# A table of the token in each slot: experts gather their rows by it and scatter finished rows to the output

## The chip, the cores and the metric

The kernel runs on one core of one Trainium2 chip. The metric is the device time of one execution in microseconds (us); the median of several executions stands for a kernel. The engines are PE (TensorE), DVE (VectorE), ACT (ScalarE), POOL (GpSimd) and SP (SyncE). SP, ACT and POOL issue DMAs. Each engine works through its own instructions in order; semaphores tie them together.

## What is computed

A layer norm of x (1250 tokens x 768), then a graph attention network (three layers, four heads) and a linear attention over the same rows; both are added to x. The change touches only what follows, a routed feed-forward layer with eight experts (F = 384):

```python
xf = layernorm(x)                                  # 1250 x 768
probs = softmax(xf @ switch_w + switch_b)          # 8 experts
prob_max, routes = max(probs), argmax(probs)
capacity = int(1.25 * N / E)                       # 195 rows an expert
rank = place of the token in its expert, by falling prob_max
keep = rank < capacity
buf[routes, rank] = xf where keep                  # 8 x 195 rows
h = gelu(buf @ w1 + b1)
o = h @ w2 + b2
y = where(keep, o[routes, rank], xf)
x = x + y * prob_max
```

## The kernel before, in words

The program is written by hand in Bass. A list `ORDER` holds (name, index) steps; each engine runs through the whole list and emits what it has to do for a step. So `ORDER` sets the order on every engine and in every DMA queue, and a wait holds up all that stands behind it on its engine. A class `Waits` leaves out waits that an engine has already passed.

The tokens are NT = 10 tiles of up to 128 rows (the last has 98). The part that matters is `last_order`. Its first part runs over the tiles in ticks, several steps of different tiles in each. In tick i SP loads `ar` (a row tile of the graph network, `row_in`) for tile i, and at i = 2, 5 and 8 also the weights `w1_in`, `w2_in` (1152 KB each) and the bias `b2_in` (384 KB) of experts 0, 1 and 2; then it loads `mi` (384 KB, `new_x`) for tile i-2. For tile t = i-2, PE ends a product in two halves (`row_mm`), DVE adds them up (`row_add`, L1477), adds `mi` (`new_x`, L1492, result in `x2`, which shares its place with `wacc`), takes mean and variance, and writes the normed row tile `xf` (L1517). PE turns `xf` in the next tick (`f_turn`, L1053) for the router (`logits`, L1062; `route`; `rank`, L1558 to L1569, which compares each token with all earlier tiles).

After the last tile comes the second part. `ranked` (L1574 to L1594) makes ten-column tables on DVE: `slot[:, 0]`, the row of `slot_rows` to which each token goes (a spare row when the expert is full), and `slot[:, 1]`, the row of `expert_rows` from which its result comes. `dispatch` has POOL scatter the ten `xf` tiles by indirect DMA into `slot_rows` in HBM (L1974), while DVE adds the token's own share to `x2` (L1599). When all ten have landed, SP loads `slot_rows` back in 13 tiles of 120 rows (`slots_in`, L2224), PE turns them (`slots_turn`, L1092), ACT evicts the low half and DVE the high half into `sT_low`, `sT_high`, and then the experts run.

For expert e, PE computes `hidden(e)` (L1104, 18 fp32 products of 195 columns), ACT applies gelu, and PE then computes `expert_out(e-1)` (L1116, 12 fp32 products of 384 columns). DVE adds b2 into `orow` (L1617), and ACT's queue stores `orow` to `expert_rows` (L1883). One or two slot tiles are turned between `expert_out(e-1)` and `hidden(e+1)`. After the last expert, `fetch` has POOL gather a row for each token from `expert_rows` (L1982); DVE scales it and adds `x2` (L1625), and SP stores the ten tiles to the output (L2228). `slot_zero` (L1888) zeroes `slot_rows` once, much earlier, on ACT's queue.

## Time and profile before

| | |
|---|---|
| median of 3 runs | 1821.16 us (1818.88 to 1825.3) |
| the profiled execution | 1823.74 us |
| its span, first to last instruction | 1822.0 us |
| PE busy | 1586.4 us (87%) |
| DVE busy | 1170.8 us (64%) |
| mean granted TensorE clock | 0.945 |

The span is what the views of the trace are measured in; 1.74 us of the execution lie outside it. The chain of work that ended last goes by 70% through PE and by 16% through DVE. The change touches the last 320 us only, so this text reads those: from 1501 us (the ticks), from 1633 us (ranking done, dispatch), from 1660 us (experts) and from 1792 us (fetch and output) to the end at 1822 us. The share of busy time over the whole span tells little about them.

### The profile page before, as it was taken

Reading aid. Unit: us, or ns where it says so; the run is one execution under the profiler, and the core shown is the slowest. Engines: PE = TensorE matmul, PEld = TensorE weight load, DVE = VectorE, ACT = ScalarE, POOL = GpSimd, SP = SyncE. Lnnn points to the kernel's source line nnn. Section 1 sums busy time; section 2 is a strip of 40 time slices with the busy share of each in tenths; the row PEclk is TensorE's granted clock in tenths of the full one; section 3 lists DMA queues with packets and bytes.
Section 4 is the critical chain, followed back from the end, with each engine's and each line's share of the span. In section 5 each row is a group of like instructions: output and inputs, shape, how many; then the busy total and the mean of one; then the engine's idle time right before and its main releaser. Section 6 shows DMA issues by size and latency. Waiting matters only on the chain.

```text
span 1822.0 us, 24680 instructions
## 1 busy us (share of the span) xinstructions
PE 1586.4 (87%) x9602; PEld 1205.0 (66%) x9663; DVE 1170.8 (64%) x2517; ACT 647.3 (36%) x1254; POOL 515.8 (28%) x282
## 2 busy tenths in 40 slices
PE   3799999999997787999998699969999998855993
PEld 2456666556565665988888688868889875534661
DVE  7677553024434697898879999968769725771113
ACT  2231111122224766766665333344324413421110
POOL 1387787777730000111211212121212210001002
PEclk9899999999998988999999899989999999967997
DMA  7424434454424315222263443444124116317615
GB/s 220 125 40 115 104 80 113 66 92 108 74 59 163 101 65 177 82 63 82 92 161 102 138 146 113 140 147 136 50 85 143 53 51 218 113 67 246 203 57 195
DMA packets 197361, 208.90 MB, mean 115 GB/s; under 512 B 83040, under 2 KB 152814, under 8 KB 197244
## 3 DMA queue, kind: packets, MB, share of 16 engines
q1 hardware_dynamic: 117453, 183.36, 30.9%
q0 software_dynamic: 76416, 14.38, 6.6%
q10 hardware_dynamic: 3375, 9.59, 2.0%
q8 instruction: 76, 1.25, 0.3%
q14 instruction: 41, 0.34, 0.1%
HBM read 140.67 MB, written 66.22 MB: 114 GB/s over the span
## 4 chain that ended last, share of the span: by engine, by line
PE 70%; DVE 16%; DMA 4%; ACT 4%; issue 3%; POOL 1%; SPq 1%; ACTq 0%; POOLq 0%; DVEq 0%
PE bank L959 17%; PE bank L805 13%; PE bank L806 13%; PE bank L804 12%; PE bank L1116 3%; PE bank L1104 3%; DVE eb L1386 3%; DVE eb L1395 2%; PE bank L984 2%; DVE junk L1349 2%; PE bank L1012 2%; ACT ef L1777 1%; PE bank L906 1%; DVE q_max L1418 1%; PE bank L1027 1%
## 5 line engine op out<-in xcount | busy, mean ns | idle before, releaser
L959 PE MATMUL bank<-hb,eb 128*128 128x193 f32 (+3 forms) x2400 | 431.3, 337 | 41.0 <-DVE eb L1395 36.0
L959 PEld LDWEIGHTS bank<-hb,eb 128*128 128x128 f32 (+3 forms) x2400 | 411.3, 195 | 53.8 <-DVE eb L1395 40.6
L1939 POOL DMA_INDIRECT table<-amount,place x170 | 342.9, 2017 | 157.7 <-DMA table<-amount,place 68.7
L1950 POOL TENSOR_TENSOR node<-node,rinv 128x960 f32<-128x960 f32 (+2 forms) x36 | 62.6, 1752 | 821.4 <-DVE rinv L1408 821.4
L1386 DVE SCALAR_TENSOR_TENSOR eb<-shift_b,as_low,shift_b 128x640 f32<-128x640 f32 (+1 forms) x240 | 231.4, 1004 | 6.9 <-DMA shift_b<-shift_rows 6.9
L1747 ACT ACTIVATE eb<-eb,asd 128x640 f32<-128x640 f32 (+1 forms) x240 | 182.6, 815 | 136.9 <-DVE eb L1386 136.9
L1395 DVE SCALAR_TENSOR_TENSOR eb<-eb,count 128x1280 f32<-128x1280 f32 (+1 forms) x120 | 200.1, 1668 | 0.0
L1349 DVE CUSTOM_DVE_ANT_0 junk<-ab,absent 128x1250 bf16<-128x1250 f32 x120 | 174.8, 1456 | 1.3
L804 PE MATMUL bank<-w_o_hi,aT_hi 128*128 128x384 bf16 (+1 forms) x360 | 120.1, 334 | 0.4 <-DVE won L1562 0.4
L805 PE MATMUL bank<-w_o_lo,aT_hi 128*128 128x384 bf16 (+1 forms) x360 | 119.8, 333 | 0.0
L806 PE MATMUL bank<-w_o_hi,aT_lo 128*128 128x384 bf16 (+1 forms) x360 | 119.7, 332 | 0.0
L804 PE MATMUL bank<-wg_hi,x1T_hi 128*128 128x384 bf16 (+3 forms) x360 | 117.9, 328 | 0.0
L806 PE MATMUL bank<-wg_hi,x1T_lo 128*128 128x384 bf16 (+3 forms) x360 | 117.9, 327 | 0.0
L805 PE MATMUL bank<-wg_lo,x1T_hi 128*128 128x384 bf16 (+3 forms) x360 | 117.8, 327 | 0.0
L1956 POOL TENSOR_TENSOR node<-node,bgh 128x960 f32<-128x960 f32 (+2 forms) x36 | 79.6, 2225 | 1.9
L1617 DVE TENSOR_TENSOR orow<-bank,b2r 105x384 f32<-105x384 f32 (+1 forms) x32 | 17.8, 556 | 94.8 <-PE bank L1116 94.8
L1777 ACT ACTIVATE ef<-bank,q_shift 128x256 f32<-128x256 f32 (+1 forms) x120 | 50.6, 476 | 73.0 <-DVE q_shift L1423 73.0
L805 PE MATMUL bank<-xnT_lo,wq_hi 128*128 128x512 bf16 (+1 forms) x210 | 70.8, 337 | 3.7 <-DVE wq_lo L1194 2.8
L806 PE MATMUL bank<-xnT_hi,wq_lo 128*128 128x512 bf16 (+1 forms) x216 | 73.0, 338 | 0.3
L1304 DVE TENSOR_REDUCE kmax<-bank 128x1 f32<-128x512 f32 (+1 forms) x60 | 40.2, 692 | 49.1 <-PE bank L806 49.1
L804 PE MATMUL bank<-xnT_hi,wq_hi 128*128 128x512 bf16 (+1 forms) x204 | 68.6, 336 | 0.0
L1012 PEld LDWEIGHTS bank<-context,qf 128*128 128x128 f32 (+1 forms) x480 | 61.5, 204 | 10.1 <-ACT att L1814 3.8
(272 smaller groups left out, 2854.4 us busy)
## 6 DMA issues: line engine op xcount, KB each, us to landing
w<-in_w SPq DMA_DIRECT2D x16, 1152.0 KB, 6.2
shift_b<-shift_rows SPq DMA_DIRECT2D x24, 625.0 KB, 6.2
h_rows<-h_row SPq DMA_DIRECT2D x27, 388.0 KB
hb<-h_rows SPq DMA_DIRECT2D x12, 873.0 KB
ar<-node_rows SPq DMA_DIRECT2D x27, 384.0 KB, 3.2
qk_rows<-qk_row SPq DMA_DIRECT2D x12, 625.0 KB
ab<-as_rows SPq DMA_DIRECT2D x12, 625.0 KB, 5.6
stage<-in_W SPq DMA_DIRECT2D x18, 384.0 KB, 4.7
```

The lines of the kernel that those rows point to most:

```text
L804: T.matmul(out_ap, lhs[0], rhs[0], start=first, stop=False, skip_group_check=skip)
L805: T.matmul(out_ap, lhs[0], rhs[1], start=False, stop=False, skip_group_check=skip)
L806: return T.matmul(out_ap, lhs[1], rhs[0], start=False, stop=last, skip_group_check=skip)
L959: ins = T.matmul(bank[w // 2][0:M, c0:c0 + GC + 1], p[0:K, u, w * P:w * P + M], hv[0:K, t, 0:GC + 1], start=opens and u == 0 and w % 2 == ...
L1012: ins = T.matmul(ov[0:R, u, hh, :], qf[q % 4][:, hh * MT + m, 0:R], context[:, m, hh, :], start=u == 0 and hh == 0 and m == 0, stop=m == M ...
L1349: V.tensor_tensor_reduce(out=junk[0:R, :], in0=ab[lh % 2][0:R, :], in1=absent[0:R, t, :], scale=1.0, scalar=-BIG, op0=ALU.add, op1=ALU.max ...
L1386: ins = V.scalar_tensor_tensor(eb[i % EDGE_BUFFERS][:, u, 0:w], low, as_low[:, t, lh:lh + 1], high, ALU.add, ALU.max)
L1395: V.scalar_tensor_tensor(e, e, 1.0, count[:, 2 * pair:2 * pair + 2, ns], ALU.min, ALU.mult).then_inc(sem["edge_w"], 1)
L1747: ins = A.activation(e[:, u, 0:w], e[:, u, 0:w], ACT.Exp, bias=asd[:, t, 8 * l + hh:8 * l + hh + 1])
L1777: ins = A.activation(ef[g % 4][0:R, hh, :], bank[3 + g % 2][0:R, hh * FEATS:(hh + 1) * FEATS], ACT.Exp, bias=bias)
L1939: G.indirect_dma_start(tables[i], bass.IndirectOffsetOnAxis(place[:, c:c + 1], axis=0), amount16[:, c:c + 1], None, compute_op=ALU.add).th ...
L1956: ins = G.tensor_tensor(v, v, bgh[lh % 2][0:R, :].unsqueeze(1).broadcast_to([R, ws.stop - ws.start, GC]), ALU.add)
```

## The change

A table in PSUM now says which token sits in each slot. DVE makes two 0/1 masks, `on_row` (128 x 10 x 105: is the token's place within its half expert this row) and `on_tile` (128 x 10 x 16: which of the 16 half experts), and multiplies the second by the token's number less 4096 and by its probability. PE multiplies and adds up over the ten tiles (`map`), which gives, for each of 105 rows and 16 half experts, the token's number less 4096 and its gate, or zeros. DVE turns these into `from_row` (clipped to a valid row), `to_row` (out of range for an empty slot) and `gate` (`mapped`).

`xf` and `x2` of each tile are stored to HBM as soon as they exist (`rows_out`, two 384 KB DMAs on SP a tile, in the tick's list behind `mi`). POOL gathers the rows of half an expert at a time straight from `xf_rows` (`slots_in`), later their `x2` rows (`base_in`), and scatters the finished rows to the output (`expert_out`). Tokens without a slot are covered by storing all of `x2` with its own share to the output first (`own`). DVE gets one more pass for each half expert. Slot tiles are now 105 and 90 rows, 16 in place of 13. The loads of the weights of experts 3 and 4 move behind `hidden(0)` in the list. `slot_zero`, `dispatch` and `fetch` are gone.

```diff
@@ last_order
+        yield "rows_out", t
...
-    yield "w1_in", 3
-    yield "w2_in", 3
-    yield "ranked", 0
-    for t in range(NT):
-        yield "dispatch", t
-    for t in range(4):
-        yield "slots_in", t
-    yield "w1_in", 4
-    yield "w2_in", 4
+    for name in ("ranked", "map", "mapped"):
+        yield name, 0
+    own = iter(range(NT))
+    for j in range(4):
+        yield "slots_in", j
+        yield "own", next(own)
     for e in range(EXPERTS + 1):
         if e < EXPERTS:
+            for j in range(2 * e, 2 * e + 2):
+                yield "slots_turn", j
+                if j + 4 < SLOT_TILES:
+                    yield "slots_in", j + 4
+                for t in itertools.islice(own, 3):
+                    yield "own", t
             yield "hidden", e
+            if e == 0:
+                for i in range(3, WEIGHT_SETS):
+                    yield "w1_in", i
+                    yield "w2_in", i
+            for j in range(2 * e, 2 * e + 2):
+                yield "base_in", j
...
@@ PE
+            def map_(_):
+                pe.wait_ge("slotted", 10)
+                pe.wait_ge("row_sum", 2 * NT * (LAYERS + 1))
+                for t in range(NT):
+                    R = rows(t)
+                    ins = T.matmul(bank[5][0:WIDEST, 0:2 * SLOT_TILES], on_row[0:R, t, :], in_tile[0:R, t, :],
+                                   start=t == 0, stop=t == NT - 1)
+                ins.then_inc(sem["map_mm"], 1)
...
@@ DVE
+                V.tensor_tensor(on_row[:, :, :], iota_row[:, :].unsqueeze(1).broadcast_to([P, NT, WIDEST]),
+                                pm[:, 5, :].unsqueeze(2).broadcast_to([P, NT, WIDEST]),
+                                ALU.is_equal).then_inc(sem["slotted"], 1)
...
+            def mapped(_):
+                at_tile, share = bank[5][0:WIDEST, 0:SLOT_TILES], bank[5][0:WIDEST, SLOT_TILES:2 * SLOT_TILES]
+                ve.wait_ge("map_mm", 1)
+                V.tensor_scalar(from_row[0:WIDEST, :], at_tile, NOWHERE + 0.25, N - 0.75, ALU.add,
+                                ALU.min).then_inc(sem["mapped"], 1)
+                V.tensor_scalar(to_row[0:WIDEST, :], at_tile, NOWHERE + 0.25, None, ALU.add).then_inc(sem["mapped"], 1)
+                V.tensor_copy(gate[0:WIDEST, :], share).then_inc(sem["mapped"], 1)
...
+                    V.scalar_tensor_tensor(orow[o][0:n, :], orow[o][0:n, :], gate[0:n, j:j + 1], base_row[j % 4][0:n, :],
+                                           ALU.mult, ALU.add).then_inc(sem["ended"], 1)
...
@@ POOL
+            def slots_in(j):
...
+                G.indirect_dma_start(sr[j % 4][0:n, :], None, xf_rows,
+                                     bass.IndirectOffsetOnAxis(from_row[0:n, j:j + 1], axis=0)
+                                     ).then_inc(sem[f"slots_in{j % 4}"], 16)
+
+            def base_in(j):
+                n = slots_of(j)[2]
+                ge.wait_ge("own_out", 16 * NT)
+                ge.wait_ge("ended", j - 3)
...
+            def expert_out(e):
+                for j in range(2 * e, 2 * e + 2):
+                    n = slots_of(j)[2]
+                    ge.wait_ge("mapped", 2)
+                    ge.wait_ge("ended", j + 1)
+                    G.indirect_dma_start(out, bass.IndirectOffsetOnAxis(to_row[0:n, j:j + 1], axis=0),
+                                         orow[j % OUT_ROWS][0:n, :], None, bounds_check=N - 1, oob_is_err=False
+                                         ).then_inc(sem[f"expert_out{j % OUT_ROWS}"], 16)
...
@@ SP
+            def rows_out(t):
+                R = rows(t)
+                sy.wait_ge("xf_ready", t + 1)
+                S.dma_start(xf_rows[at(t), :], xf[0:R, t, :]).then_inc(sem["rows_out"], 16)
+                S.dma_start(x2_rows[at(t), :], x2[0:R, t, :]).then_inc(sem["rows_out"], 16)
```

SP's queue at the tick that loads expert 1's weights. Before (`ar_99` is tile 5's, `w_1` the two weights, the last row tile 3's `mi`):

```order
L2164 DMA ar_98<-node_rows 128x768 [waits turned]
L2219 DMA mi_153<-mixed_rows 128x768 [waits x2]
L2164 DMA ar_99<-node_rows 128x768 [waits turned]
L2200 DMA w_1_219<-in_w 128x6x384
L2207 DMA w_1_220<-in_w 128x3x768
L2212 DMA b2r_223<-in_b 128x768
L2219 DMA mi_154<-mixed_rows 128x768 [waits x2]
```

And now:

```order
L2255 DMA mi_159<-mixed_rows 128x768 [waits x2]
L2260 DMA xf_rows<-xf 128x768 [waits xf_ready]
L2261 DMA x_rows<-wacc 128x768
L2202 DMA ar_103<-node_rows 128x768 [waits turned]
L2236 DMA w_1_229<-in_w 128x6x384
L2243 DMA w_1_230<-in_w 128x3x768
L2248 DMA b2r_233<-in_b 128x768
L2255 DMA mi_160<-mixed_rows 128x768 [waits x2]
```

The loads of a tick now stand behind a store that waits for `xf` of tile t-1, and `mi` of tile t is the last of them.

DVE around expert 1's rows and the slot copies that follow them. Before:

```order
L1617 TENSOR_TENSOR orow_239<-bank,b2r_223 105x384 [waits out2_mm,b2_in1]
L1617 TENSOR_TENSOR orow_239<-bank,b2r_223 105x384 [waits out2_mm]
L1617 TENSOR_TENSOR orow_240<-bank,b2r_223 90x384 [waits out2_mm] x2
L1605 COPY sT_high<-bank 128x3x120 [waits slots_turned] x2
```

And now:

```order
L1657 TENSOR_TENSOR orow_249<-bank,b2r_233 105x384 [waits out2_mm,b2_in1]
L1657 TENSOR_TENSOR orow_249<-bank,b2r_233 105x384 [waits out2_mm]
L1663 SCALAR_TENSOR_TENSOR orow_249<-orow_249,gate,base_row_115 105x768 [waits base_in2,expert_row]
L1657 TENSOR_TENSOR orow_250<-bank,b2r_233 90x384 [waits out2_mm] x2
L1663 SCALAR_TENSOR_TENSOR orow_250<-orow_250,gate,base_row_116 90x768 [waits base_in3,expert_row]
L1645 COPY sT_high<-bank 128x3x105 [waits slots_turned]
L1645 COPY sT_high<-bank 128x3x90 [waits slots_turned]
```

A full-width pass now stands between the last `orow` addition and the first slot copy, and there are always two slot copies.

## Rows read from the trace of the kernel before

**Rows 1.** Chain of waits, 1500 to 1560 us: start, us, what
```profile
1501.42 0.32 SPq L2164
...
1514.06 0.97 DVE wacc L1492
...
1518.57 1.51 PE bank L1053 x6
...
1524.59 0.97 DVE wacc L1492
```

**Rows 2.** Timeline of DVE, 1495 to 1634 us: x2 added, xf written
```profile
1528.27 0.68 DVE L1517 TENSOR_SCALAR xf<-wacc,stats 128x768 f32<-128x768 f32 x1
1534.23 0.96 DVE L1492 SCALAR_TENSOR_TENSOR wacc<-wacc,mi 128x768 f32<-128x768 f32 x1
1537.91 0.68 DVE L1517 TENSOR_SCALAR xf<-wacc,stats 128x768 f32<-128x768 f32 x1
1544.40 0.96 DVE L1492 SCALAR_TENSOR_TENSOR wacc<-wacc,mi 128x768 f32<-128x768 f32 x1
1568.98 0.68 DVE L1517 TENSOR_SCALAR xf<-wacc,stats 128x768 f32<-128x768 f32 x1
1576.14 0.96 DVE L1492 SCALAR_TENSOR_TENSOR wacc<-wacc,mi 128x768 f32<-128x768 f32 x1
```

**Rows 3.** Timeline of SP's DMA issues, tick that loads expert 2's weights
```profile
1556.05 0.32 SPq L2164 DMA_DIRECT2D ar<-node_rows  x1
```

**Rows 4.** Tile mi, issue to landing: load issued at 1515.05, then at 1558.01 us
```profile
DMA to landing us min/median/max: 2.8/2.8/2.8
...
DMA to landing us min/median/max: 8.9/8.9/8.9
```

**Rows 5.** Windows: length, PE, PEld, DVE, ACT, POOL busy, PEclk, DMA share, GB/s
```profile
1562.00:1564.00 2.00, 2.00 (x14) 1.18 (x13) 1.42 (x5) 1.01 (x1) 0.00 (x0) 1.00 1.03 418
1754.00:1756.00 2.00, 2.00 (x8) 2.00 (x7) 0.00 (x0) 0.00 (x0) 0.00 (x0) 0.50 0.01 5
```

**Rows 6.** Chain of waits, 1560 to 1822 us
```profile
1623.41 2.02 PE bank L1062 x12
...
1633.02 0.20 DVE pm L1574
...
1649.54 3.34 DMA slot_rows<-xf,slot
...
1660.20 8.67 PE bank L1104 x36
...
1677.48 7.75 PE bank L1116 x24
...
1686.74 6.21 PE bank L1104 x36
1692.95 7.75 PE bank L1116 x24
...
1703.82 6.18 PE bank L1104 x36
...
1753.46 7.86 PE bank L1104 x36
...
1776.79 15.49 PE bank L1116 x48
...
1808.41 7.96 DMA sr<-expert_rows,slot
```

**Rows 7.** Timeline, 1629 to 1825 us
```profile
1634.89 9.38 DVE L1599 SCALAR_TENSOR_TENSOR wacc<-xf,pm,wacc 128x768 f32<-128x768 f32 x10
1635.14 1.68 POOL L1974 DMA_INDIRECT slot_rows<-xf,slot  x1 [143.84 <-DVE pm L1594]
...
1796.30 1.00 POOL L1982 DMA_INDIRECT got<-expert_rows,slot  x1 [145.80 <-DMA expert_rows<-orow]
...
1800.25 1.02 DVE L1625 SCALAR_TENSOR_TENSOR got<-got,pm,wacc 128x768 f32<-128x768 f32 x1 [7.39 <-DMA got<-expert_rows,slot]
```

More of the change, by code:

```diff
@@ L424, in last_order @@
                 yield "b2_in", e - 1 + 3
-    for t in range(NT):
-        yield "fetch", t
 def whole_order():
@@ L502, in program @@
         attn_rows = dram("attn_rows", (N, D))
[L503 to L504 removed]
+        xf_rows = dram("xf_rows", (N, D))
+        x2_rows = dram("x2_rows", (N, D))
         base = 16512
@@ L544, in program @@
         pm = put("pm", [P, 8, NT])
-        slot = put("slot", [P, 2, NT], U32)
         b1c = put("b1c", [128, EXPERTS, KF])
@@ L553, in program @@
         b2r = [put("b2r0", [128, D])]
+        iota_row = put("iota_row", [P, WIDEST])
+        to_row, from_row = (put(name, [P, SLOT_TILES], U32) for name in ("to_row", "from_row"))
+        gate = put("gate", [P, SLOT_TILES])
         assert cursor[0] <= after_count
+        cursor[0] = at_logits
+        iota_i = put("iota_i", [P, WIDEST], I32)
         r_a = cursor[0] = after_count
@@ L572, in program @@
         cursor[0] = r_a
-        w1_3, w2_3 = put("w1_3", [128, KD, F]), put("w2_3", [128, KF, D])
-        sr = [put(f"sr{i}", [P, D]) for i in range(4)]
+        sT_high = put("sT_high", [128, KD // 2, SLOTS])
+        sr = [put(f"sr{i}", [P, D]) for i in range(3)]
         assert cursor[0] <= r_b
@@ L580, in program @@
         r_c = cursor[0]
+        cursor[0] = r_b
+        base_row = [put(f"base_row{i}", [P, D]) for i in range(4)]
         cursor[0] = r_b
@@ L712, in program @@
         assert cursor[0] <= over
-        cursor[0] = r_d
-        got = [put(f"got{i}", [P, D]) for i in range(6)] + sr
-        assert cursor[0] <= after_features
+        cursor[0] = r_zero
+        sr.append(put("sr3", [P, D]))
         identP = ident[0:P, 0:P]
@@ L1633, in vector_program @@
                         expert_setup=expert_setup, new_x=new_x, new_norm=new_norm, logits=logits, route=route,
-                        rank=rank, ranked=ranked, dispatch=dispatch, slots_turn=slots_turn,
-                        expert_out=expert_out, fetch=fetch_)
+                        rank=rank, ranked=ranked, mapped=mapped, own=own_, slots_turn=slots_turn,
+                        expert_out=expert_out)
             for name, *where in ORDER:
@@ L1968, in expert_setup @@
                                 pattern=[[-1, P]], channel_multiplier=1).then_inc(sem["pool_set"], 1)
-            def dispatch(t):
-                R = rows(t)
-                ge.wait_ge("slotted", 10)
-                ge.wait_ge("slot_zeroed", 16)
-                G.indirect_dma_start(slot_rows, bass.IndirectOffsetOnAxis(slot[0:R, 0, t:t + 1], axis=0),
-                                     xf[0:R, t, :], None).then_inc(sem["to_slots"], 16)
-            def fetch_(t):
-                R = rows(t)
-                for o in range(OUT_ROWS):
-                    ge.wait_ge(f"expert_out{o}", 16 * (2 * EXPERTS // OUT_ROWS))
-                ge.wait_ge("hid_mm", KF * EXPERTS)
-                G.indirect_dma_start(got[t][0:R, :], None, expert_rows,
-                                     bass.IndirectOffsetOnAxis(slot[0:R, 1, t:t + 1], axis=0)
-                                     ).then_inc(sem[f"fetch{t}"], 16)
+            def slots_in(j):
+                n = slots_of(j)[2]
+                ge.wait_ge("rows_out", 32 * NT)
+                ge.wait_ge("mapped", 1)
+                ge.wait_ge("slots_turned", 2 * (j - 3))
+                G.indirect_dma_start(sr[j % 4][0:n, :], None, xf_rows,
+                                     bass.IndirectOffsetOnAxis(from_row[0:n, j:j + 1], axis=0)
+                                     ).then_inc(sem[f"slots_in{j % 4}"], 16)
@@ L1986, in gpsimd_program @@
             mine = dict(edges_in=edges_in, place=place_, finish=finish,
-                        expert_setup=expert_setup, dispatch=dispatch, fetch=fetch_)
+                        expert_setup=expert_setup, slots_in=slots_in, base_in=base_in, expert_out=expert_out)
             for name, *where in ORDER:
@@ L2238, in sync_program @@
                     mine[name](*where)
-            sy.wait_ge("result_out", 16 * NT)
+            sy.wait_ge("own_out", 16 * NT)
+            for o in range(OUT_ROWS):
+                sy.wait_ge(f"expert_out{o}", 16 * (SLOT_TILES // OUT_ROWS))
         block = ctx.enter_context(nc.Block())
```

157 lines of the change are left out of this document (76 added, 81 removed).

## The prediction

> **What bounds the kernel now.** I read the page's chain first (PE 70%), then the chain of waits, the timeline and the windows of the last 320 us, since the change touches nothing before. There are four stretches, each with another bound.
>
> In the ticks (1501 to 1620 us) DVE and PE hand work to each other and neither has slack: x2 of a tile, xf, PE's turn, the ranking, the next product. Whatever delays x2 delays everything. The reader should see that this happens once already: `mi` of tile 0 stands behind expert 0's weights in SP's queue, its tick began with an issue at 1501.42 and DVE got the tile at 1514.06, 12.5 us later; PE turned xf at 1518.57 [rows 1]. At expert 2's tick issue to landing took 1556.05 to 1558.01 + 8.9 = 1566.9, that is 10.9 us [rows 3, 4], but nobody waited: the tile was needed at 1576.14 [rows 2].
>
> From 1633.0 the dispatch is a single file: tables, ten scatters, a landing, a load, turns, then `hidden(0)` at 1660.2 [rows 6]. From there PE bounds with gaps between experts, up to 1776.79 + 15.49 = 1792.3 [rows 6]. Then 29.7 us of fetch and output up to 1822.0, in which PE does nothing.
>
> **The end: -24.0 us.** Now, after PE's last product: DVE's addition of 0.6, one more pass (the same form over 768 columns took 1.02 [rows 7]), a hand-over of 0.3 (DVE's tables to POOL's first scatter), then one indirect scatter of 90 rows. The last scatter of before took 3.34 us from the start of its instruction to landing [rows 6]. Sum 0.6 + 1.0 + 0.3 + 3.4 = 5.3, with 0.4 for the end of the program 5.7 against 29.7: -24.0. Bounds: the scatter lands in 2.5 or in 5.0 us, so -25 to -22.5.
>
> **The dispatch: -9.7 us.** From the tables' start at 1633.0 [rows 6]: six small DVE steps, 1.1 us; the mask of 1050 columns 1.2 us (768 columns took 0.96, so 1.25 ns a column [rows 2]); three shorter passes, 0.8 us; ten products for the table. Twelve records of six router products took 2.02 us at the low clock [rows 6], 0.34 us each, so 3.4 us for ten. Then `from_row` and the hand-over, 0.6. POOL starts its first gather at 1640.1. The first gather of before was used 3.95 us after its start (1796.30 to 1800.25 [rows 7]), so rows are there at 1644.1. The turn takes 1.5, the second tile comes 1.3 to 1.9 later. What bounds then is DVE, in its order: own shares 0 to 3, slot copy 0, own shares 4 to 6, slot copy 1. An own share costs 0.94 (9.38 for ten [rows 7]), so copy 0 ends at 1646.4, the three shares at 1649.2, copy 1 at 1649.8. With a little for gathers that meet the 3.8 MB of stores of the own shares, `hidden(0)` starts at 1650.5 in place of 1660.2. Bounds -11 to -8.
>
> **The first product: +1.0 us.** `hidden(0)` took 8.67 where others take 6.2 [rows 6], because PE came out of a wait at 1.2 GHz. Before, 3.6 us of turns ran without a break ahead of it; now they are thinner and DVE makes PE wait 2 to 3 us after them. I take +1.0; bounds 0, and all of it at the low clock, 12.4, so +3.7.
>
> **The gaps between experts: +6.6 us.** Before, a gap with one slot tile is 1677.48 + 7.75 = 1685.23 to 1686.74, 1.5 us; with two it is 1692.95 + 7.75 = 1700.70 to 1703.82, 3.1 us [rows 6]. There were three of each among the six: 13.9 us. ACT's wait for its store, which held up its slot copy, is gone. But on DVE the added pass stands between the last `orow` and the first slot copy: 0.6 + 1.0 + 0.5, then the second tile's high half is turned, 0.6, and copied, 0.45, with hand-overs 3.4 us, and every gap has two tiles. Six times 3.4 is 20.5: +6.6, bounds +5 to +8. POOL's three DMAs a half expert, 48 of 1.0 to 1.7 us [rows 7], lie beside 110 us of products; base rows are asked for a whole expert ahead, so nobody waits.
>
> **The clock in the gaps: +1.7 us.** One gap of three of 3.1 us was followed by a fall to the low clock (0.50 at 1754 to 1756 [rows 5]): 7.86 in place of 6.2 [rows 6]. Six gaps at one in three give two falls, one more than before. Bounds: no fall, -1.7, and six, +8.3.
>
> **The ticks: +16.9 us.** This is the part that speaks against the change. `mi` of tile t now stands behind the two stores of tile t-1, so it can't be asked for before xf of t-1 is written; before, tile 6's was asked for at 1558.01, 11.6 us ahead of that and 18 us before its use [rows 2, 4]. What is left is the time from the end of xf to the next L1492: 1538.59 to 1544.40 = 5.8 for tile 3, 1569.66 to 1576.14 = 6.5 for tile 6, 1528.95 to 1534.23 = 5.3 for tile 2 [rows 2]. In an ordinary tick four DMAs of 0.39 MB stand in the queue (two stores, `ar`, `mi`): 1.57 MB at some 0.41 MB/us (418 GB/s at best [rows 5]) take 3.9; a lone `mi` took 2.8, of which 1.0 is data [rows 4], so 1.8 + 3.9 = 5.8 to 6.0. That just fits; I take 0.8 in all for tile 2 and its like, bounds 0 and 4.
>
> At the ticks of experts 1 and 2 the weights stand ahead of `mi` as well. Before, such a queue took 10.9 to 12.5 us [rows 1, 3, 4]; the stores put 0.79 MB in front, 1.9 us: 12.8 to 14.4 from the end of xf. DVE then waits 12.9 - 5.8 = 7.1 (up to 8.7) at tile 3 and 12.9 - 6.5 = 6.4 (up to 8.0) at tile 6. I take 7.4 + 6.7 = 14.1, near the lower ends, since the shorter time is the one measured in mid-stage. Bounds 12 and 17. Expert 0's tick stays as it is. In addition PE idles over 6 us, as in tile 0's tick, where the time to the next x2 was 1524.59 - 1514.06 = 10.5 against 9.6 for the one after [rows 1, 2] although it had less ranking in it. I take 1.5 at tile 3 and 0.5 at tile 6, where the clock falls anyway: +2.0, bounds 0 and 5. Once a tick is late nothing later gives it back.
>
> The trace shows 418 GB/s in such a stretch [rows 5]. The Trainium skill ("DMA: Bandwidth & Descriptors", Specifications) gives about 358 GB/s as a core's share of HBM; by that figure the same queues would take 1.5 us longer each and the sum would be 3 us worse. The trace disagrees with the figure, so the sum goes by the trace.
>
> The zeroing of `slot_rows` at 914 us goes as well. It costs ACT one issue beside a stretch that PE bounds: 0, at most -0.6. The last stores of the ticks land 15 us before the first gather asks for them, so they are hidden.
>
> **Sum.** -24.0 - 9.7 + 1.0 + 6.6 + 1.7 + 16.9 = -7.5 us. On the profiled execution that is 1823.74 - 7.5 = 1816.2; that execution was 2.6 above the median, and against 1821.16 it is 1813.7, rounded to 1814. A measurement of this kernel can tell about 0.3%, 5.5 us, from no change. All lower bounds together give some -21, all upper ones +15; independent as they are, the case holds 1806 to 1823.
>
> **Rivals.** *The ticks hide it.* If stores and loads overlap, or `mi` doesn't wait its turn behind the weights, the 16.9 us are not there: -24.4, 1797. The 12.5 and 8.9 us landings of `mi` against 2.8 alone speak against it [rows 1, 4]. Chance 0.13.
>
> *The clock eats it: slower.* Every gap is now longer than the longest of before. If PE drops to 1.2 GHz in each of the six (+8.3 in place of +1.7), does all of `hidden(0)` there (+3.7 in place of +1.0) and pays 2.9 at both late ticks (+5.8 in place of +2.0), the sum is -7.5 + 13.1 = +5.6: 1827. It decides once the three clock terms, 4.7 in the forecast, exceed 12.2. For it: one gap of three did fall. Against: the other two didn't, with gaps only 0.3 us shorter. The Trainium skill ("TensorE: Matmul & The Clock Gate", HAM oscillation) describes a kernel whose waits bring the clock down at every step; the trace bears that out for one gap in three. Chance 0.14.
>
> *The indirect DMAs don't deliver.* If first gather and last scatter take the 7.96 us of the last fetch, which met other traffic [rows 6], in place of 3.95 and 3.34, the start loses 4.0 and the end 4.6: -7.5 + 8.6 = +1.1, 1822. For it: the gather meets the own shares' stores. Against: at the end the queues are empty. Chance 0.13.
>
> **Chances.** Forecast 0.60, the rivals 0.13, 0.14, 0.13. Faster by over 0.3% (below 1815.7): 0.37 of the forecast and the first rival, 0.50. Within: 0.22 of the forecast, 0.11 of the third, 0.02 of the second, 0.35. Slower: 0.15. The range leaves out most of the first rival and a tail on top: 1801 to 1828.
>
> **What would show it.** DVE waiting 6 to 8 us for `mi` ahead of x2 of tiles 3 and 6, and no wait above 1.5 at the others; SP's `mi` issues 1 to 3 us after xf. `hidden(0)` some 17 us after the tables' start in place of 27. Gaps of 3.4 us between experts, ended by DVE's slot copy, not ACT's. The end 5 to 6 us after PE's last product. I am wrong if those waits for `mi` are missing (then far faster), or if low-clock windows follow every gap.

## The result, and the profile after

The changed kernel took 1814.19 us (median of 8 runs, 1810.71 to 1816.3) against 1820.3 us for the kernel before on the same chip (8 runs; its first three gave the 1821.16 of above). The ratio is 0.9965, 95% interval 0.9951 to 0.9978: faster by 6.1 us, a third of a per cent. The forecast was 1814, and the case it named, slightly faster, is what came. Run once more on another chip it gave 0.9969 [0.9952, 0.9986].

| | before | after |
|---|---|---|
| median | 1820.3 us | 1814.19 us |
| the profiled execution | 1823.74 us | 1810.71 us |
| its span | 1822.0 us | 1809.0 us |
| PE busy | 1586.4 us | 1595.9 us |
| DVE busy | 1170.8 us | 1179.4 us |
| mean granted TensorE clock | 0.945 | 0.949 |

The two profiled executions lie 13 us apart where the medians lie 6.1 apart. 4.3 us of that come from the stretch ahead of the change: its last eviction of `node` starts at 1479.1 us before and at 1474.8 after, and over the fourteen profiles of this study that start lies between 1470.8 and 1485.2, whatever the kernel. From that eviction to the end of the span is 342.9 us before and 334.2 after. This **tail** holds all that the change touches, and it is far steadier than the whole: in three more profiles with the same work in it (the changed kernel again, `x_zero` and `x_mark` below) it is 334.0, 334.0 and 333.9. So the change is worth 8.7 us in the tail. That the medians give 6.1 to 5.6 agrees with it: the interval of the first measurement goes from 4.0 to 8.9 us. It may also be that the one profile of before has a tail a little above its usual; this stays open.

The chain of waits of the changed kernel, 1640 to 1809 us (start, us, what), answers to [rows 6]:

```profile
1646.40 0.20 DVE pm L1597
...
1647.46 1.25 DVE on_row L1612
...
1654.42 1.14 POOL sr L2003
...
1655.87 7.03 DMA sr<-xf_rows,from_row
...
1664.97 9.22 PE bank L1125 x36
...
1682.54 7.75 PE bank L1137 x24
...
1690.32 0.56 DVE orow L1657
...
1690.91 1.01 DVE orow L1663
1691.92 0.41 DVE sT_high L1645
...
1693.40 6.18 PE bank L1125 x36
...
1784.81 15.49 PE bank L1137 x48
```

The tables begin at 1646.40 where they began at 1633.02; `hidden(0)` follows 18.6 us later where it took 27.2; a gap between experts now runs from 1682.54 + 7.75 = 1690.29 to 1693.40, 3.1 us, and what ends it is DVE's slot copy behind the new pass; PE's last product ends at 1800.3, and the span 8.7 us after it.

The timeline of DVE answers to [rows 2]. Columns: start, us, engine, line, operation, tiles, and in brackets the idle time ahead of it and what ended it. These are x2 of tiles 0, 2, 3 and 6:

```profile
1509.36 0.96 DVE L1514 SCALAR_TENSOR_TENSOR wacc<-wacc,mi 128x768 f32<-128x768 f32 x1 [3.96 <-DMA mi<-mixed_rows]
1530.49 0.96 DVE L1514 SCALAR_TENSOR_TENSOR wacc<-wacc,mi 128x768 f32<-128x768 f32 x1 [0.89 <-DMA mi<-mixed_rows]
1534.17 0.68 DVE L1539 TENSOR_SCALAR xf<-wacc,stats 128x768 f32<-128x768 f32 x1
1548.43 0.96 DVE L1514 SCALAR_TENSOR_TENSOR wacc<-wacc,mi 128x768 f32<-128x768 f32 x1 [7.81 <-DMA mi<-mixed_rows]
1590.11 0.96 DVE L1514 SCALAR_TENSOR_TENSOR wacc<-wacc,mi 128x768 f32<-128x768 f32 x1 [8.28 <-DMA mi<-mixed_rows]
```

And SP's timeline in the tick that loads expert 1's weights, which answers to [rows 3]:

```profile
1534.88 0.32 SPq L2260 DMA_DIRECT2D xf_rows<-xf  x1
1535.24 0.43 SPq L2261 DMA_DIRECT2D x_rows<-wacc  x1
1535.72 0.48 SPq L2202 DMA_DIRECT2D ar<-node_rows  x1
1536.24 0.94 SPq L2236 DMA_DIRECT2D w<-in_w  x1
1537.23 0.83 SPq L2243 DMA_DIRECT2D w<-in_w  x1
1538.10 0.50 SPq L2248 DMA_DIRECT2D b2r<-in_b  x1
1538.64 0.49 SPq L2255 DMA_DIRECT2D mi<-mixed_rows  x1
```

Here is the price of the change in seven lines. `xf` of tile 2 is written at 1534.17 + 0.68 = 1534.85; within 0.03 us SP starts its first store, and only then can it issue the loads; `mi` is the last, at 1538.64; and DVE gets it at 1548.43, 13.6 us after `xf`. Waits of 7.8 and 8.3 us stand at tiles 3 and 6, where the kernel before had none.

### The profile page after: what moved, and what is told of

Read it like the earlier page. It is cut to its first block, busy times and chain, and to the rows that moved or that the text cites. A ratio compares the mean times of both kernels' runs of the same rounds, so it can differ in the third digit from the quotient of the medians.

```text
span 1809.0 us, 24889 instructions
## 1 busy us (share of the span) xinstructions
PE 1595.9 (88%) x9701; PEld 1208.5 (67%) x9701; DVE 1179.4 (65%) x2532; ACT 647.5 (36%) x1257; POOL 538.8 (30%) x311
## 4 chain that ended last, share of the span: by engine, by line
PE 71%; DVE 16%; DMA 4%; ACT 3%; issue 3%; SPq 1%; POOL 0%; POOLq 0%; DVEq 0%; ACTq 0%
PE bank L971 17%; PE bank L816 13%; PE bank L818 13%; PE bank L817 13%; PE bank L1137 3%; PE bank L1125 3%; DVE eb L1407 3%; PE bank L996 2%; DVE eb L1416 2%; PE bank L1024 2%; DVE junk L1370 2%; DMA mi<-mixed_rows 2%; PE bank L918 1%; DVE q_max L1439 1%; ACT ef L1815 1%
## 5 line engine op out<-in xcount | busy, mean ns | idle before, releaser
L816 PE MATMUL bank<-xnT_hi,wq_hi 128*128 128x512 bf16 (+1 forms) x216 | 73.1, 338 | 2.4 <-DVE wq_lo L1215 2.4
L1657 DVE TENSOR_TENSOR orow<-bank,b2r 105x384 f32<-105x384 f32 (+1 forms) x32 | 17.8, 556 | 82.8 <-PE bank L1137 82.8
L1024 PEld LDWEIGHTS bank<-context,qf 128*128 128x128 f32 (+1 forms) x480 | 62.1, 206 | 10.3 <-ACT att L1852 3.8
```

The lines of the kernel that those rows point to most:

```text
L816: T.matmul(out_ap, lhs[0], rhs[0], start=first, stop=False, skip_group_check=skip)
L1024: ins = T.matmul(ov[0:R, u, hh, :], qf[q % 4][:, hh * MT + m, 0:R], context[:, m, hh, :], start=u == 0 and hh == 0 and m == 0, stop=m == M ...
```

## The experiments

All kernels are the changed one with the edit shown. Each was compared with the kernel before on the same chip; three groups of four ran on three chips, where the kernel before took 1823.98, 1822.09 and 1820.69 us. Since whole times of one kernel scatter by several us, I give the tail too.

| kernel | median us (runs) | ratio to before, 95% | tail us | tail to before |
|---|---|---|---|---|
| before | | 1 | 342.9 | |
| changed | 1814.19 (8) | 0.9965 [0.9951, 0.9978] | 334.2 | -8.7 |
| `again` | 1815.5 (12) | 0.9969 [0.9952, 0.9986] | 334.0 | -8.9 |
| `x_zero` | 1817.3 (10) | 0.9957 [0.9941, 0.9974] | 334.0 | -8.9 |
| `x_behind` | 1795.16 (4) | 0.9856 [0.9824, 0.9888] | 317.1 | -25.8 |
| `x_bytes` | 1811.69 (5) | 0.9932 [0.9906, 0.9959] | 330.7 | -12.2 |
| `x_wlast` | 1792.48 (4) | 0.9855 [0.984, 0.987] | 313.2 | -29.7 |
| `x_own` | 1814.75 (7) | 0.9956 [0.9936, 0.9976] | 333.3 | -9.6 |
| `x_last` | 1806.29 (7) | 0.9923 [0.9896, 0.995] | 329.2 | -13.7 |
| `x_plain` | 1809.58 (1) | | 330.4 | -12.5 |
| `x_mark` | 1819.08 (1) | | 333.9 | -9.0 |
| `x_all` | 1786.94 (6) | 0.9825 [0.9793, 0.9857] | 307.7 | -35.2 |
| `x_best` | 1778.93 (5) | 0.977 [0.9748, 0.9791] | 297.9 | -45.0 |
| `x_best_zero` | 1780.81 (5) | 0.9788 [0.977, 0.9805] | 300.1 | -42.8 |

### The ticks: is it the wait, the bytes, or the weights in between?

The theory was that the late `mi` comes from the order of SP's queue: the stores wait for `xf`, the loads stand behind them, and the weights stand ahead of `mi`. One rival was that the 0.79 MB of stores simply fill the DMA engines, so that they would cost the same wherever they are issued.

**Stores of tile t-1 issued behind `mi` of tile t.** Same bytes, no loads behind a wait.

```diff
-        yield "rows_out", t
+        if t:
+            yield "rows_out", t - 1
...
+    yield "rows_out", NT - 1
```

> The stores of xf and x2 of tile t-1 stand behind mi of tile t in SP's queue, one tick later than in the changed kernel; nothing else differs. My theory: mi is late there because its issue waits for xf of the tile before and the stores' bytes stand ahead of it. Then mi of tiles 3 and 6 is asked for a tick earlier and DVE's waits of 7.8 and 8.3 us go, the 0.9 at tile 2 too, with the low clock after them: 15 to 18 us off the changed kernel's 1814.2, so 1797 to 1799. Rival (the DMA engines are simply full in those ticks, whatever the order): the waits stay above 4 us each and the time above 1808.

Measured: 0.9856, tail -25.8, which is 17.1 less than the changed kernel's. Of the `mi` waits only that of tile 0 is left (5.67 us; the kernel before has 4.31 there); x2 of tile 3 and of the tile behind it in DVE's timeline, both without idle time ahead of them:

```profile
1543.24 0.96 DVE L1516 SCALAR_TENSOR_TENSOR wacc<-wacc,mi 128x768 f32<-128x768 f32 x1
1553.55 0.96 DVE L1516 SCALAR_TENSOR_TENSOR wacc<-wacc,mi 128x768 f32<-128x768 f32 x1
```

The bytes are all still there, so the bandwidth rival falls: 17 of the change's 17.7 us in the ticks come from the place of the stores in the queue.

**The wait left, the stores behind.** SP still waits for `xf` of tile t ahead of the next loads, but the stores are issued behind `mi`.

```diff
-        yield "rows_out", t
+        if t:
+            yield "rows_out", t - 1
+        yield "rows_wait", t
...
+            def rows_wait(t):
+                sy.wait_ge("xf_ready", t + 1)
```

> SP still waits for xf of tile t before it issues the loads of the next tick, but the two stores themselves come a tick later, behind mi. It takes apart what makes mi late: the wait (issue at xf's end) or the 0.79 MB of stores ahead of it. If the sum of the prediction is right, the wait carries 10.9 of 12.8 us and the bytes 1.9: DVE's waits of 7.8 and 8.3 us fall to about 6, the 0.9 at tile 2 goes, 4 to 5 us off: 1809 to 1811. Rival (the stores' bytes are what hurts): waits near 0, as in the run that moves the whole step.

Measured: 0.9932, tail -12.2. The waits at tiles 3 and 6:

```profile
1553.68 0.96 DVE L1517 SCALAR_TENSOR_TENSOR wacc<-wacc,mi 128x768 f32<-128x768 f32 x1 [6.79 <-DMA mi<-mixed_rows]
1593.28 0.96 DVE L1517 SCALAR_TENSOR_TENSOR wacc<-wacc,mi 128x768 f32<-128x768 f32 x1 [7.00 <-DMA mi<-mixed_rows]
```

From x2 of tile 0 to x2 of tile 6 it takes 76.7 us, where the changed kernel takes 80.8 and `x_behind` 63.0: of the 17.8 us between these two, the bytes that stand ahead of `mi` are worth 4.1 and the late issue 13.7. (I go by this stretch here, since the tail also holds a fall of the clock behind one gap between experts, +1.6 us, and a first product shorter by 1.4.) So most of the cost comes from SP's wait for `xf`, not from what is stored; the waits were expected to fall to about 6 us and fell to 6.8 and 7.0. The forecast had split a late tick into 10.9 to 12.5 us of queue and 1.9 of stores; here the stores are worth 1.0 and 1.3 us a tick (7.81 - 6.79 and 8.28 - 7.00), and the small wait at tile 2 goes as well.

**The weights behind `mi`.** The stores stay where the change put them; the weights and bias of experts 0 to 2 go behind the `mi` of the same tick.

```diff
     def loads(t):
         yield "row_in", u0 + t
-        if t in (2, 5, 8):
-            yield "w1_in", t // 3
-            yield "w2_in", t // 3
-            yield "b2_in", t // 3
...
         yield "new_x", t
+        if t in (0, 3, 6):
+            yield "w1_in", t // 3
+            yield "w2_in", t // 3
+            yield "b2_in", t // 3
```

> The changed kernel with its stores where they are; only the weights and bias of experts 0, 1 and 2 stand behind mi of their tick, not ahead of it. If the late mi is the sum of both (issued after xf, and 2.75 MB of weights ahead), an ordinary tick's queue remains for tiles 3 and 6: the waits of 7.8 and 8.3 us fall to 0 to 1, tile 0's wait of 4 to 5 us goes too, with some low clock: 18 to 22 us off the changed kernel's 1815 (6 below the kernel before), so 24 to 28 below the kernel before. Rival (the wait for xf alone makes mi late): 5 us off at most, from tile 0.

Measured: 0.9855, tail -29.7. x2 of tiles 0 to 6, of which I show 0, 1 and 3:

```profile
1501.49 0.96 DVE L1514 SCALAR_TENSOR_TENSOR wacc<-wacc,mi 128x768 f32<-128x768 f32 x1
1511.97 0.96 DVE L1514 SCALAR_TENSOR_TENSOR wacc<-wacc,mi 128x768 f32<-128x768 f32 x1 [1.60 <-DMA mi<-mixed_rows]
...
1533.11 0.96 DVE L1514 SCALAR_TENSOR_TENSOR wacc<-wacc,mi 128x768 f32<-128x768 f32 x1 [0.32 <-DMA mi<-mixed_rows]
```

The wait for `xf` stands in SP's queue as before, in every tick, and costs at most 1.6 us at one tile (4.0 over all seven). So the late issue hurts only where 2.7 MB stand between it and `mi` (behind tile 0, 3 and 6 the weights are now issued ahead of SP's next wait, and the `mi` after them was late by 1.60, 0.92 and 0.34 us). It takes both: a queue held back until `xf` is written, and a large load ahead of the small one that is needed first. Taking away either gives 17 to 21 us. `x_wlast` gives more since it also frees tile 0, which stood behind expert 0's weights in both kernels [rows 1]. The kernel before could have had that part too: no run here moves the weights in it, so the distance of `x_wlast` and of `x_best` below to the kernel before isn't all due to the table of slots.

By the same stretch the kernel before takes 1576.14 - 1514.06 = 62.1 us [rows 1, 2], the changed one 1590.11 - 1509.36 = 80.8, and `x_wlast` 64.3.

### The dispatch: what slows the first gather?

In the changed kernel PE uses the rows of the first gather 1659.90 - 1654.42 = 5.5 us after its start and those of the second after 7.0; the forecast had 3.95, with "a little" for the own shares' stores. To tell whether those stores are to blame, SP's stores of the own shares wait for the first four gathers.

```diff
             def own_(t):
+                for b in range(4):
+                    sy.wait_ge(f"slots_in{b}", 16)
                 sy.wait_ge("own", t + 1)
```

> SP stores the tokens' own shares only when the first four gathers have landed. In the changed kernel the second gather took 7.0 us from its start to PE's turn, the first 5.5. If the ten stores of own shares slow the gathers, both fall to about 4, the second tile is turned at some 6 us after POOL's first start in place of 8.5, and hidden(0) starts 2 us earlier: 1812. DVE's three own shares between the two slot copies then bound. Rival (the gathers are slow by themselves): no change, 1814.

Measured: 0.9956, tail -9.6; the chain of waits of `x_own`:

```profile
1658.21 1.14 POOL sr L2003
...
1659.66 4.08 DMA sr<-xf_rows,from_row
...
1667.28 8.43 PE bank L1125 x36
```

PE's turns of the two tiles in its timeline, first in the changed kernel and then in `x_own`:

```profile
1659.90 1.31 PE L1113 MATMUL bank<-ident,sr 105*128 105x105 f32 x6 [6.56 <-DMA sr<-xf_rows,from_row]
1662.94 1.16 PE L1113 MATMUL bank<-ident,sr 90*128 90x90 f32 x6 [1.73 <-DMA sr<-xf_rows,from_row]
```

```profile
1662.21 1.31 PE L1113 MATMUL bank<-ident,sr 105*128 105x105 f32 x6 [5.08 <-DMA sr<-xf_rows,from_row]
1663.79 1.16 PE L1113 MATMUL bank<-ident,sr 90*128 90x90 f32 x6 [0.26 <-DMA sr<-xf_rows,from_row]
```

In both kernels the chain goes by the second gather (1655.87 and 1659.66), and its wait falls from 7.03 to 4.08 us; the first gather's time from start to use falls from 5.5 to 1662.21 - 1658.21 = 4.0. So the stores are what slows the gathers. But from `from_row` to `hidden(0)` it gives only 1.5 us, 11.6 to 10.1, since DVE's own shares then stand ahead of its slot copies, as the forecast had it. In this profile one gap of six was followed by a fall of the clock (the product at 1694.92 took 7.87 us in place of 6.2), which eats most of the gain; the tail shows 0.7 to 0.9 of it where 2 were expected, and in the ratio it can't be told from nothing. `x_all` below moves DVE's six later own shares behind both slot copies too, and comes to 8.4 us.

### The gaps: DVE's pass ahead of the slot copies

```diff
+            if e > 1:
+                yield "ended", e - 2
             yield "hidden", e
...
-                    V.scalar_tensor_tensor(...).then_inc(sem["ended"], 1)
+                    if part == 0:
+                        ended_row(2 * e)
...
+            def ended(e):
+                ended_row(2 * e + 1)
```

The pass for the second half of an expert goes behind the next expert's slot copies.

> DVE's pass that ends an expert's second half (add the gated row to the base row) comes behind the two slot copies of the next expert in place of ahead of them. In the changed kernel a gap between experts is 3.1 us and holds orow 0.56, the pass 1.01, a slot copy 0.41, a turn, a copy. If that pass is what the added time in the gaps is, each of the six gaps falls by about 0.9 to 2.2 and the time by 5 to 6 us against the changed kernel. Rival (ACT's copy or the turns take over as what is late): gaps of 2.8 and 2 us off at most.

Measured: 0.9923, tail -13.7, 5.0 less than the changed kernel's. A gap of `x_last` in the chain of waits:

```profile
1701.93 7.74 PE bank L1142 x24
1709.67 0.29 PE bank L1118 x3
...
1709.98 0.44 ACT sT_low L1917
...
1710.56 0.44 PE bank L1118 x3
...
1711.02 0.41 ACT sT_low L1917
...
1711.83 4.20 PE bank L1130 x24
```

1709.67 to 1711.83 is 2.2 us against 3.1, and DVE has left the chain; ACT's copy of the second tile ends the gap. Six times 0.95 is 5.7 us, and from the end of `hidden(0)` to the end of PE's last product it is 5.8 (126.1 to 120.3). That the tail shows 5.0 is chance in other stretches: a first product shorter by 1.2 us and ticks longer by 2.1. The last scatter's issue and the end are as they were.

### The end: why 8.7 us and not 5.7?

The forecast let the last scatter land 3.4 us after its start and the program end 0.4 us later. In the changed kernel POOL starts it at 1802.77 and the span ends at 1809.0, 6.2 us later. Either the scatter is slow to complete, or something else holds the end.

**The last 90 rows by SP, with a plain store.**

```diff
-                for j in range(2 * e, 2 * e + 2):
+                for j in range(2 * e, min(2 * e + 2, SLOT_TILES - 1)):
                     n = slots_of(j)[2]
                     ge.wait_ge("mapped", 2)
...
+            sy.wait_ge("ended", SLOT_TILES)
+            S.dma_start(spare_rows[0:90, :], orow[3][0:90, :]).then_inc(sem["own_out"], 16)
```

> The last half expert's 90 rows are stored by SP with a plain DMA into rows that nobody reads, not scattered by POOL, so those rows of the output lack the expert's share. In the changed kernel the last scatter's bytes moved 3.8 to 5.2 us after PE's end, and the span ended 8.7 after it, 3 us more than predicted. If an indirect DMA from POOL has that tail in its completion or in POOL's own end, the span ends 5 to 6 us after PE's last product here, 3 us less. If the tail belongs to the end of any program or to stores to HBM, it stays at 8 to 9.

Measured (one run): PE's last product ends at 1787.26 + 15.49 = 1802.75 and the span at 1807.7, 5.0 us, against 8.7. The plain store is issued at 1804.41 and all is over 3.3 us later. But the last indirect scatter that is left starts at 1801.37, and the end comes 6.3 us after that one as well, so this run alone leaves both readings open.

**A mark behind the last scatter.** SP waits until all scatters have completed, and then stores 16 rows to a spare place.

```diff
                 sy.wait_ge(f"expert_out{o}", 16 * (SLOT_TILES // OUT_ROWS))
+            S.dma_start(spare_rows[0:16, 0:D], orow[3][0:16, :]).then_inc(sem["own_out"], 16)
+            sy.wait_ge("own_out", 16 * NT + 16)
```

> The changed kernel; after SP has waited for the last scatters it issues one small plain store, whose issue time shows when the last scatter's completion came. The span ended 6.2 us after POOL began the last scatter in every kernel so far, also in the one whose last 90 rows went by SP. If completion is as quick as the old dispatch's (3.3 us), the mark is issued 3.3 us after POOL's start and the span ends at 6.2 all the same or with the mark: the rest is POOL's own way out of the program. If completion itself is slow, the mark comes at about 6 us and the span ends 2 us later than before, 8.

Measured (one run): timeline of POOL and of SP, and the windows of the end (length; PE, PEld, DVE, ACT, POOL busy; clock, DMA share, GB/s):

```profile
1811.06 0.94 POOL L2021 DMA_INDIRECT out_x<-orow,to_row  x1 [2.90 <-DVE orow L1664]
```

```profile
1814.33 0.32 SPq L2280 DMA_DIRECT2D spare_rows<-orow  x1
```

```profile
1812.00:1813.00 1.00, 0.00 (x0) 0.00 (x0) 0.00 (x0) 0.00 (x0) 0.00 (x1) 0.81 0.53 135
1813.00:1814.00 1.00, 0.00 (x0) 0.00 (x0) 0.00 (x0) 0.00 (x0) 0.00 (x0) 0.50 0.39 141
1814.00:1815.00 1.00, 0.00 (x0) 0.00 (x0) 0.00 (x0) 0.00 (x0) 0.00 (x0) 0.50 0.00 0
1815.00:1816.00 1.00, 0.00 (x0) 0.00 (x0) 0.00 (x0) 0.00 (x0) 0.00 (x0) 0.50 0.26 49
1816.00:1817.00 1.00, 0.00 (x0) 0.00 (x0) 0.00 (x0) 0.00 (x0) 0.00 (x0) 0.50 0.00 0
```

The scatter starts at 1811.06, its bytes move until 1814, and SP has seen its completion 3.3 us after the start, the size the forecast took. Then there is room for a whole further store, issued at 1814.33 and moving its bytes between 1815 and 1816, and the span still ends at 1817.2, 6.1 us after the scatter's start. In the eleven other profiles that end with this scatter the distance is 6.15 to 6.25 us, and 6.33 in `x_plain` from its own last one. So the scatter isn't slow. It landed as forecast, and 2.9 us later the program ended.

```profile
L481 POOLq DRAIN  x1: 6198/6198/6198, 1802.5 to 1802.5; - x1
L481 SPq DRAIN  x1: 7/7/7, 1806.2 to 1806.2; - x1
L481 SPq EVENT_SEMAPHORE  x1: 17/17/17, 1808.9 to 1808.9; - x1
```

And in `x_plain`:

```profile
L481 POOLq DRAIN  x1: 6387/6387/6387, 1801.1 to 1801.1; - x1
L481 SPq DRAIN  x1: 7/7/7, 1807.1 to 1807.1; - x1
```

POOL's DRAIN ends at 1808.7 in the changed kernel, 2.5 us after SP's, and the span ends 0.2 us behind it. In `x_mark` it ends at 1810.8 + 6.2 = 1817.0, and SP, extra store and all, was through at 1816.2. In `x_plain` it ends at 1807.5, still 0.4 us behind SP's: there too POOL holds the end, and the gain is that its last scatter starts earlier. DVE's DRAIN ends with DVE's last pass (1802.0 in the changed kernel), but POOL's goes on for 5.0 us after POOL's last scatter instruction, in twelve of the thirteen profiles, and for 5.2 in `x_plain`. It isn't a fixed time either: in the kernel before, whose last gather took 7.96 us to its use, POOL's DRAIN ended 8.6 us after that instruction, at 1818.0, 4.0 us ahead of the span's end; there SP's last four plain stores, issued from 1813.25 on over 4.5 us, held the end. What in POOL the DRAIN waits for, 2.7 us beyond the completion that SP saw, no run here tells.

### The zeroing

```diff
+        if i == 3 * ITEMS:
+            yield "slot_zero", 0
...
+            def slot_zero(_):
+                se.wait_ge("set_up", 1)
+                A.dma_start(zero_rows[...], zero[...]).then_inc(sem["slot_zeroed"], 16)
```

The 4.8 MB of zeros put back in their old place, into a region that nothing reads; POOL's first gather waits for them, as the first scatter did.

> The zeroing of 4.8 MB on ACT's queue at about 914 us is put back into the changed kernel, into rows that nobody reads. The profiled executions differ by 4.3 us ahead of the ticks, 3.0 of it between 800 and 970 us. If the zeroing had a price, the time is 3 to 4 us longer, 1817 to 1818, and the ticks start 3 to 4 us later. If that is scatter between executions, it stays at 1814 within 1.5, as predicted (at most 0.6).

Measured: 0.9957, as the changed kernel within the intervals; tail 334.0, and from the first to the last eviction of `node` (764.9 to 1485.2) 720.3 us. That number looked at first like a cost of the zeroing, since before has 720.1 and after 716.6. But `x_bytes` and `x_best`, without zeroing, have 720.2 and 720.0, and `x_best_zero`, with it, has 712.0. The median of 1817.3 is also what the expectation gave for a price, but the kernel before took 1823.98 on that chip, and the ratio is even a little lower than without the zeroing. `x_best_zero` against `x_best` gives 1780.81 against 1778.93 with intervals that overlap: 1.9 us slower, between the two readings of its expectation, and of the other sign. The removal of the zeroing is worth nothing that can be measured here.

> The changed kernel itself once more, beside the others of this call on the same chip, since the runs with one part changed so far shared a chip on which the kernel before took 1824. Every theory expects the ratio of the first measurement, 0.9965, that is 6 us below the kernel before; it is the base for the other three.

`again` is the changed kernel itself, run beside the second group. It shows the same picture: waits for `mi` of 5.08, 1.15, 7.68 and 7.72 us, gaps of 3.1, no fall of the clock in them, and 8.7 us from PE's last product to the end.

### All together

`x_all` joins `x_behind`, `x_last` and `x_own` with DVE's own shares moved: 

```diff
-                for t in itertools.islice(own, 3):
-                    yield "own", t
+            for t in itertools.islice(own, 6):
+                yield "own", t
+            if e > 1:
+                yield "ended", e - 2
```

> Three things together: the stores of xf and x2 behind the next tick's mi; the stores of own shares only after the first four gathers, with DVE's own shares 4 to 9 behind both slot copies; and DVE's last pass of an expert behind the next slot copies. By what each is worth in my reading: 18 for the ticks, 3 to 4 ahead of hidden(0), 5 to 6 in the gaps: 26 to 28 us off the changed kernel, 1786 to 1789 where that takes 1814. If the gaps don't shrink and the first product just starts colder, 20 us, 1794.

Measured: 0.9825, tail -35.2, which is 26.5 less than the changed kernel's; the parts alone give 17.1 and 5.0, which leaves 4.4 for the own shares; 3.2 of that show between the tables and `hidden(0)` (18.6 to 15.3). Its chain of waits from `from_row` to `hidden(0)` takes 1644.10 - 1635.73 = 8.4 us; every gap is 2.2.

> All three parts of the combined kernel (36 us below the kernel before) and the weights behind mi. Only tile 0's wait of 5.2 us is left for that to remove, with the low clock behind it: 5 to 7 us more, 41 to 43 below the kernel before, 1779 to 1781 where that takes 1822. Rival: tile 0 then waits on something else (its row product), 2 us at most.

`x_best` is `x_all` with the weights behind `mi`. Measured: 0.977, 95% interval 0.9748 to 0.9791, 42 us below the kernel before and 35 below the changed one. The tail is 297.9 us, 9.8 less than that of `x_all`: 5.2 up to x2 of tile 0, 2.8 from there to x2 of tile 1, and 1.7 between tiles 7 and 8, which `x_best_zero` doesn't show. It beats both kernels. The start of its experts in the chain of waits:

```profile
1636.55 1.14 POOL sr L2017
...
1637.99 4.09 DMA sr<-xf_rows,from_row
...
1643.87 9.01 PE bank L1132 x36
...
1661.21 7.74 PE bank L1144 x24
...
1671.10 6.18 PE bank L1132 x36
```

> The same with the 4.8 MB zeroing put back at 914 us, beside it on the same chip. Of the profiles so far, the stretch from the first to the last eviction of the graph network took 720 us in the two kernels that zero and 715, 717, 717 and 720 in four that don't. If the zeroing costs, this is 2 to 3 us slower than the one without; if the difference is scatter, within 1.

Its result stands above, under the zeroing.

## Why the prediction was right, point by point

| term | forecast | in the profiles |
|---|---|---|
| ahead of the ticks | 0 | -4.35, scatter |
| the ticks | +16.9 | 149.33 - 131.60 = +17.7 |
| the dispatch | -9.7 | 18.57 - 27.18 = -8.6 |
| the first product | +1.0 | 9.22 - 8.67 = +0.55 |
| gaps and their clock | +6.6 + 1.7 | 126.11 - 123.40 = +2.7 |
| the end | -24.0 | 8.70 - 29.73 = -21.0 |
| sum from the ticks on | -7.5 | -8.65 |

The stretches run from SP's first issue of the ticks (1501.42 before, 1497.07 after) to the tables (1633.02, 1646.40), to `hidden(0)` (1660.20, 1664.97), to the end of PE's last product (1792.27, 1800.30) and to the end. The sum was 1.2 us off; two of its terms were off by 3 and by 5.6 in opposite directions, so the exactness is luck, while the sign and the rough size of each term but the clock's were right. Luck is also in the margin: the medians moved by 6.1 us, where 5.5 was the least that was taken to be told from no change.

**The ticks** held in mechanism and nearly in size. DVE was forecast to wait 7.1 to 8.7 us at tile 3 and 6.4 to 8.0 at tile 6, and waited 7.81 and 8.28; tile 2 was forecast at 0.8 and took 0.89. From the end of `xf` to the next x2 it was to be 12.8 to 14.4 us and was 13.6 at tile 3 and 14.7 at tile 6. (The upper end came from tile 0, whose rows give 12.6 where the prediction wrote 12.5.) That I took the lower ends put tile 6 1.6 us short. The runs bear out how it was reckoned, the time of the queue from `xf` on less the 5.3 to 6.5 us that DVE has work for: `x_wlast` shows that without the weights in it the queue nearly fits into that time, and `x_bytes` that without the stores' bytes most of it stays (they were worth 1.0 and 1.3 us, not 1.9). The 2.0 us for the clock came out as 1.1: from x2 of tile 3 to the next it took 1.7 us more than before and from that of tile 6 to the next 1.1 more, but from tile 7 to tile 8 it took 11.34 in place of 13.02, since the low clock of before (0.74 and 0.50 from 1596 to 1600 us) had no counterpart there. So something did give time back.

**The dispatch** was 1.1 us short, within its bounds (-11 to -8), and 0.9 of that were lost ahead of the first gather: it started 8.0 us after the tables began, not 7.1. `on_row` took 1.25 (forecast 1.2), the map's products 3.75 (3.4), and `from_row` with the hand-over to POOL 1654.42 - 1653.35 = 1.1 (0.6). From there to `hidden(0)` it took 10.5 us (10.4), though the gathers took 5.5 and 7.0 us in place of some 4, by `x_own` because of the stores of the own shares. The "little" for that, 0.7, was half of the 1.5 us that `x_own` saves, and DVE's work was reckoned 0.6 too long. The price of a gather beside no store was right: 4.0 us from its start to its use in `x_own`.

**The first product** came at 9.22 us, within its bounds; over the thirteen profiles of this study's kernels it is anything from 7.8 to 9.2.

**The gaps** were mis-sized: 3.1 us each and not 3.4, which is +4.7 for the six where +6.6 stood, just under the bound of +5; and as a sum with the clock +2.7 where +8.3 stood. The forecast took three short and three long gaps of before, and one fall among them; the fall of before (7.86 us at 1753.46) had no counterpart after, so the clock term was 0 - 1.7 = -1.7 in place of +1.7, which was its lower bound. With that, six gaps at 3.1 are 18.7 against 14.0, +4.7, less 1.7 for the clock, +3.0; the pause between `hidden(0)` and `hidden(1)`, which the forecast left out, is 0.3 us shorter (2.43 to 2.15). Nine profiles have six gaps of 3.1 us each. In six of them no product behind such a gap is slow; in the other three (`x_own`, `x_bytes`, `x_mark`) exactly one is, 7.8 to 7.9 us, and it is the first each time. Those three are also the ones whose first product was short (8.4, 7.8, 7.9 us against 9.1 to 9.2 in the six), so what is saved at the one place is paid at the other; why, no run here tells. With gaps of 2.2 us there was no fall in four profiles, one of them (`x_last`) with a first product of 8.0. The Trainium skill ("TensorE: Matmul & The Clock Gate", HAM oscillation) describes kernels whose pauses bring the clock down over and over. Here three of 54 gaps of 3.1 us did; the rival that rested on a fall in each gap (1827) was wrong.

**The end** was 3.0 us too good, outside its bounds (-25 to -22.5). The completion of the scatter was right (3.3 us from its start), DVE's two steps were right (0.57 and 1.03), but the hand-over from DVE to POOL took 1802.77 - 1801.94 = 0.83 in place of 0.3, and the end of the program came 2.9 us after the completion in place of 0.4, for which the prediction names no row. This was the step that failed: [rows 6, 7] show what a scatter costs in mid-program, and none of them shows a program that ends with one. POOL's closing DRAIN stands in that place, 5.0 us from the end of the last scatter's instruction.

**The zeroing** at nothing: confirmed within what can be measured.

**The rivals.** "The ticks hide it" would have been 1797. It is wrong for the kernel as changed, and its time is that of `x_behind`, 1795, for the reason it would have needed: loads that don't wait. "The indirect DMAs don't deliver" was right at the start, where the gathers took 1.5 and 3.0 us more beside the stores, of which 1.5 us reached `hidden(0)`. At the end it was wrong in its reason: the scatter landed in 3.3 us, and the 3.0 us that were missing came from the hand-over and from POOL's DRAIN.

## What to carry to other kernels

A store put into a queue of loads brings its wait with it: everything behind it is issued only when the stored tile is ready, and a large load between that wait and a small urgent one makes the delay visible. Issue a tile's stores behind the next tile's urgent loads, and large prefetches behind both; either alone was worth 17 to 21 us here, two to three times what the whole change brought. When the execution time scatters by more than the effect, compare the stretch that the change touches: the tail of four profiles agreed within 0.3 us while their spans differed by 10.

## What the runs showed of the hardware that I had not expected

In all thirteen profiles of the changed kernel and its variants the span ends 6.1 to 6.3 us after POOL starts its last indirect DMA, though in `x_mark` SP saw that DMA complete after 3.3 us and a further small store fitted in between: POOL's closing DRAIN ends 5.0 to 5.2 us after POOL's last instruction, and the other engines leave the program only then. Two indirect gathers, of 105 and 90 rows of 3 KB, took 4.0 and 4.1 us from start to use with no store beside them, and 5.5 and 7.0 beside plain stores of 3.8 MB. From the end of the DVE instruction that POOL waits for to the start of its indirect DMA it took 0.3 us at the first scatter of the kernel before (1634.85 to 1635.14) and 0.9 and 0.8 at the first gather and the last scatter of the changed one (1653.55 to 1654.42, 1801.94 to 1802.77). The stretch from the first to the last eviction of `node`, which no edit here touches, takes between 712.0 and 720.3 us from one profile to the next, 8.3 us, about what the whole change is worth (6.1 in the medians, 8.7 in the tail).
